# Expert weights split by pairs in three equal blocks beside the attention, with a third query buffer and unrolled heads

## The chip, the core and the metric

The kernel runs on one core of a Trainium2 chip (trn2). The metric is the device time of one launch in microseconds (us), lower is better. TensorE is PE in the profile, VectorE is DVE, ScalarE is ACT, GpSimd is POOL, and SyncE is SP. SP only issues DMAs here. All outputs are float32.

## What is computed

The model has four parts in a row, each behind a layernorm and with a residual sum: attention, a mixture of 32 experts, a state space layer and a feed forward layer with weights from a table. The change lies in the first part, which also prepares the weights of the second:

```python
# attention, x is (2, 1024, 512), 16 heads of 32
q = jnp.einsum('btc,hcd->bhtd', x, Wq) + bq[None, :, None, :]
k = jnp.einsum('btc,hcd->bhtd', x, Wk) + bk[None, :, None, :]
v = jnp.einsum('btc,hcd->bhtd', x, Wv) + bv[None, :, None, :]
scores = jnp.einsum('bhtd,bhsd->bhts', q, k) * scale
probs = jax.nn.softmax(scores + causal, axis=-1)
y = jnp.einsum('bhts,bhsd->bhtd', probs, v)
return y.transpose(0, 2, 1, 3).reshape(Bn, Tn, H * D) @ Wo + bo
# experts, 32 of them, 8 per token, inner size 192
g = jnp.einsum('th,eih->tei', x, w_gate_proj)
u = jnp.einsum('th,eih->tei', x, w_up_proj)
h = jax.nn.silu(g) * u * masked_w[:, :, None]
out = jnp.einsum('tei,ehi->th', h, w_down_proj)
```

To keep float32 accuracy on TensorE, a matrix is split into a high part (rounded to the fp32r type) and a low part (what is left). The expert weights need this once each, and that is the work that GpSimd does during the attention.

## The kernel before

The launch is a row of stages, and each is a block in which every engine has its own program. A stage ends when all its engines have ended. `attention` (L226) has three: `norm_and_project` (layernorm, then q, k and v; the parts of q and k go to DRAM), `attend` (L491, all 16 heads) and `output_projection` (L893). Only `attend` changes, apart from the order in which the host lays out the expert weights.

**TensorE, VectorE and ScalarE in `attend`.** A unit is a head, with both batches. A body is two heads, and the engines loop over six of the eight bodies; the first and the last are written out. For a head TensorE computes the scores twice. In `rows` (L709) a token's scores lie along the free dimension of the PSUM tile `ps_r`, and VectorE takes their maximum (L838). In `columns` (L739) the scores lie turned, in `ps_c`, and ScalarE takes the exponential of them (L808). Between the two, the maxima are joined and split by VectorE (L846, L850, L852), turned by TensorE (L720, L728) and put into spare rows of the query tile `q_st` by ScalarE (L797), so that the second product comes with the maximum subtracted. `output` (L752) multiplies by V into `ps_y`, and VectorE copies that to `y_st` in two halves of 512 tokens (`evacuate`, L860). The rows of head u+1 run between the columns of head u, so TensorE is a head ahead with them. There are 24 pieces of each kind in a head.

**SyncE.** It loads q and k of head u+2 into the same two buffers while head u runs, in four steps: low half of q after four of the twelve column steps, low half of k after eight (`after_column`), upper halves of both after the last. Each step is two DMAs, one of 64 partitions and one of 32. Then it waits until both halves of y are in `y_st` and stores them (`store`, L667 and L668, four DMAs). VectorE waits for all four before it writes the first half of the next head (`y_stored`). SyncE also loads the output weights `wo` ahead of the last body (L690).

**GpSimd.** It goes through the 32 experts, two for each head. For one expert it

- splits gate and up: a cast of 128x1536 to the high part (L588), a subtraction for the low part (L591), a store of both to DRAM (L594, 1536 KB), a load of the same part of the expert after next (L567, 768 KB),
- splits down: two casts of 128x512 (L607, L608), a subtraction (L611), a subtraction on the lower 64 partitions, whose rows hold the 64 rest rows of the expert a second time (L614), a store (L617, 768 KB), a load (L570, 512 KB).

Ahead of the two experts of a head it copies V of this head into `v_pair` (`take_v`, L577), once TensorE has ended the head before the last. After the last expert it splits `wo` (L637, L640) and waits for its stores. All these DMAs are issued by GpSimd itself, in order with its arithmetic.

The order on each engine is that of the code. DMAs of GpSimd run in queue q0, those of SyncE in q1.

Of the kernel before, what the change touches and what calls it, by code (L numbers as in the profile page):

```python
# [6 lines left out]
F32 = mybir.dt.float32  # L7
I32 = mybir.dt.int32
ALU = mybir.AluOpType
# [3 lines left out]
P = 128  # L13
N_TOK = 2048
D = 512
# [475 lines left out]
def attend(nc, qk, v_rows, yT, all_sums, w_raw, w_split, wo, wo_hi, wo_lo):  # L491
# [13 lines left out]
    RING = 4  # L505
    BUFS = 3
# [3 lines left out]
    GU, DN = W_GU, W_RAW - W_GU  # L510
# [3 lines left out]
    with ExitStack() as ctx:  # L514
        sb = lambda n, s, dt=F32: ctx.enter_context(nc.sbuf_tensor(n, s, dt))
        q_st, k_st = [sb(f"q_st{b}", [P, BATCH, T], F32R) for b in range(E)], [sb(f"k_st{b}", [P, BATCH, T], F32R) for b in range(E)]
        v_pair = [sb(f"v_pair{b}", [P, TILES, VW]) for b in range(E)]
        probs = [[sb(f"probs{a}{b}", [P, HALF]) for b in range(RING)] for a in range(BATCH)]
        y_st, raw_wo = sb("y_st", [P, T]), sb("raw_wo", [P, KD, D])
# [5 lines left out]
        raw_gu, raw_dn = [sb(f"e_raw_gu{x}", [P, GU]) for x in range(2)], [sb(f"e_raw_dn{x}", [P, DN]) for x in range(2)]  # L525
        gu_parts, dn_parts = [sb(f"e_gu_parts{x}", [P, 2 * GU], F32R) for x in range(2)], sb("e_dn_parts", [P, 3 * D], F32R)
# [4 lines left out]
        low_loaded, q_up_loaded, k_up_loaded = [[sem(f"{n}_loaded{b}") for b in range(E)] for n in ("qk_low", "q_up", "k_up")]  # L531
        consts, rows_done, max_done, joined, parts_done, turned, shift_ready, cols_done, exp_done, v_ready, pv_done, y_done, y_stored, turns_begun, loads_begun, warmed = [
            sem(n) for n in ("att_consts", "rows_done", "max_done", "max_joined", "max_parts_done", "max_turned", "shift_ready", "cols_done", "exp_done", "v_ready",
                             "pv_done", "y_done", "y_stored", "v_turns_begun", "q_loads_begun", "exp_warmed")]
        gu_loaded, dn_loaded = [sem(f"e_gu_loaded{x}") for x in range(2)], [sem(f"e_dn_loaded{x}") for x in range(2)]
        gu_stored, dn_stored = [sem(f"e_gu_stored{x}") for x in range(2)], sem("e_dn_stored")
        gu_split, dn_split = sem("e_gu_split"), sem("e_dn_split")
# [7 lines left out]
        def _(pool):  # L545
# [4 lines left out]
            pool.memset(raw_gu[0][:, :T], 0.0).then_inc(consts, 1)  # L550
            pool.memset(raw_gu[1][:, :T], 1.0).then_inc(consts, 1)
# [3 lines left out]
            pool.affine_select(out=raw_gu[1][:, :T], in_=raw_gu[1][:, :T], compare_op=ALU.is_ge, fill=0.0,  # L555
# [8 lines left out]
            start = lambda it, e: isinstance(it, int) and it == 0 and e == 0  # L564

            def load_gu(p, x):
                pool.dma_start(raw_gu[x][:, :], w_raw[bass.ds(p, 1), :, :GU].rearrange("e p c -> p (e c)")).then_inc(gu_loaded[x], 16)  # L567

            def load_dn(p, x):
                pool.dma_start(raw_dn[x][:, :], w_raw[bass.ds(p, 1), :, GU:].rearrange("e p c -> p (e c)")).then_inc(dn_loaded[x], 16)  # L570

            def take_v(it, e):
                u = unit(it, e)
                if not (isinstance(it, int) and it == 0):
                    pool.wait_ge(pv_done, (u - 1) * PER_UNIT + BATCH * RING)
                    pool.sem_inc(turns_begun, 1)
                nc.gpsimd.tensor_copy(v_pair[e][:, :, :DH], v_rows[:, :, bass.ds(u * DH, DH)]).then_inc(v_ready, 1)  # L577

            def split_gate_up(it, e, x, final):
                u = unit(it, e)  # L580
                p = u * 2 + x
                hi = gu_parts[x][:, :GU]
                pool.wait_ge(gu_loaded[x], u * 16 + 16)
                pool.sem_inc(turns_begun, 1)
                if not start(it, e):
                    pool.wait_ge(gu_stored[x], u * 16)
                    pool.sem_inc(turns_begun, 1)
                nc.gpsimd.tensor_copy(hi, raw_gu[x][:, :]).then_inc(gu_split, 1)  # L588
                pool.wait_ge(gu_split, p * 2 + 1)
                pool.sem_inc(turns_begun, 1)  # L590
                nc.gpsimd.tensor_tensor(gu_parts[x][:, GU:], raw_gu[x][:, :], hi.bitcast(F32), ALU.subtract).then_inc(gu_split, 1)  # L591
                pool.wait_ge(gu_split, p * 2 + 2)
                pool.sem_inc(turns_begun, 1)
                pool.dma_start(w_split[bass.ds(p, 1), :, :2 * GU].rearrange("e p c -> p (e c)"), gu_parts[x][:, :].bitcast(F32)).then_inc(gu_stored[x], 16)  # L594
                if not final:
                    load_gu(p + 2, x)

            def split_down(it, e, x, final):
                u = unit(it, e)
                p = u * 2 + x  # L600
                hi, lo, rest = dn_parts[:, :D], dn_parts[:, D:2 * D], dn_parts[:, 2 * D:]
                pool.wait_ge(dn_loaded[x], u * 16 + 16)
                pool.sem_inc(turns_begun, 1)
                if not (start(it, e) and x == 0):
                    pool.wait_ge(dn_stored, p * 16)
                    pool.sem_inc(turns_begun, 1)
                nc.gpsimd.tensor_copy(rest, raw_dn[x][:, D:]).then_inc(dn_split, 1)  # L607
                nc.gpsimd.tensor_copy(hi, raw_dn[x][:, :D]).then_inc(dn_split, 1)  # L608
                pool.wait_ge(dn_split, p * 4 + 2)
                pool.sem_inc(turns_begun, 1)  # L610
                nc.gpsimd.tensor_tensor(lo, raw_dn[x][:, :D], hi.bitcast(F32), ALU.subtract).then_inc(dn_split, 1)  # L611
                pool.wait_ge(dn_split, p * 4 + 3)
                pool.sem_inc(turns_begun, 1)
                nc.gpsimd.tensor_tensor(rest[REST_E:, :], raw_dn[x][REST_E:, D:], rest[REST_E:, :].bitcast(F32), ALU.subtract).then_inc(dn_split, 1)  # L614
                pool.wait_ge(dn_split, p * 4 + 4)
                pool.sem_inc(turns_begun, 1)
                pool.dma_start(w_split[bass.ds(p, 1), :, 2 * GU:].rearrange("e p c -> p (e c)"), dn_parts[:, :].bitcast(F32)).then_inc(dn_stored, 16)  # L617
                if not final:
                    load_dn(p + 2, x)

            def body(it, final):
                for e in range(E):
                    take_v(it, e)
                    for x in range(2):
                        split_gate_up(it, e, x, final and e == E - 1)
                        split_down(it, e, x, final and e == E - 1)

            for x in range(2):
                load_gu(x, x)
                load_dn(x, x)  # L630
            body(0, False)
            with pool.Fori(1, BODIES - 1) as it:
                body(it, False)
            body(BODIES - 1, True)
            pool.wait_ge(wo_loaded, 16)
            pool.sem_inc(turns_begun, 1)
            nc.gpsimd.tensor_copy(wo_hi[:, :, :], raw_wo[:, :, :]).then_inc(wo_split, 1)  # L637
            pool.wait_ge(wo_split, 1)
            pool.sem_inc(turns_begun, 1)
            nc.gpsimd.tensor_tensor(wo_lo[:, :, :], raw_wo[:, :, :], wo_hi[:, :, :].bitcast(F32), ALU.subtract).then_inc(wo_split, 1)  # L640
            for x in range(2):
                pool.wait_ge(gu_stored[x], 16 * HEADS)
# [2151 lines left out]
```

## Times and profile before

| | us |
|---|---|
| median of three runs | 2579.88 (2578.06 to 2584.63) |
| the profiled execution | 2575.64 |
| its span in the profile | 2574.1 |
| `attend`, first instruction of GpSimd to the end of its last | 172.2 to 628.5 |
| first instruction of `output_projection` on SyncE | 631.3 |
| granted TensorE clock over the whole span | 0.945 |

The profile shows one execution. A row of the timeline gives start, length, engine, line, operation, output and input, how many instructions are merged in it, and in brackets how long the engine sat idle before it and who ended that. A row of the waits gives who waited for whom, the sum, the count and the longest. A row of the stretches gives its length and the busy time of each engine in it with the count of instructions, then the granted clock (1.00 is 2.4 GHz, 0.50 is 1.2 GHz), the mean busy share of the 16 DMA engines and the bytes that they moved per second.

### The profile page before, as it was taken

To read this page: it belongs to the slowest core of one execution; us is meant where nothing else is said; L and a number is where in the kernel's file an instruction comes from. 1 tells how busy PE (TensorE), PEld (TensorE's weight loads), DVE (VectorE), ACT (ScalarE), POOL (GpSimd) and SP (SyncE) were. 2 spreads that over 40 slices of the span, in tenths; PEclk is the share of its full clock that TensorE was granted. 3 is DMA by queue.
4 is the path that set the end of the run, shared out by engine and by line. 5 is a ranking of instruction groups with operands and counts; after the bars stand their busy time and mean duration, and the time that the engine had idled before them with its cause. 6 is when DMAs were issued, how large, how long until landed. Compare 5 with 4: busy or idle time off the path is not lost. (4 is left out here: it accounts for less than half of the span.)

```text
span 2574.1 us, 47582 instructions
## 1 busy us (share of the span) xinstructions
PE 2334.5 (91%) x12710; PEld 1773.7 (69%) x12712; DVE 1497.5 (58%) x3155; ACT 977.3 (38%) x2202; POOL 1094.5 (43%) x993
## 2 busy tenths in 40 slices
PE   7969998996756999999999779999989998999998
PEld 5855455443535989989989648888855664788886
DVE  6336556663566555555555457999256665655554
ACT  3114555453254444444444342222255553312221
POOL 3128888776002666666667501111166663000000
PEclk9978999998866999999999879999999999999999
DMA  5458999996355999999999834447499761000001
GB/s 178 122 175 311 346 338 329 341 326 252 116 204 145 245 283 281 258 265 273 271 263 221 149 129 148 168 163 232 141 217 225 166 151 38 13 25 25 25 9 66
DMA packets 263307, 491.18 MB, mean 191 GB/s; under 512 B 31889, under 2 KB 149137, under 8 KB 253458
## 3 DMA queue, kind: packets, MB, share of 16 engines
q1 hardware_dynamic: 197202, 272.17, 34.9%
q0 software_dynamic: 62976, 212.42, 29.4%
q10 hardware_dynamic: 3024, 5.29, 0.6%
q8 instruction: 54, 0.88, 0.1%
q14 instruction: 51, 0.42, 0.1%
HBM read 592.96 MB, written 198.79 MB: 308 GB/s over the span
## 5 line engine op out<-in xcount | busy, mean ns | idle before, releaser
L1431 PE MATMUL m_ps_u<-m_ring,m_xT_hi 128*128 x1280 | 370.4, 350 | 0.2 <-issue 0.2
L1399 POOL DMA_INDIRECT expert_sum<-x_res,token_of x160 | 257.1, 1607 | 182.9 <-DMA expert_sum<-x_res,token_of 66.3
L808 ACT ACTIVATE probs<-ps_c 128x512 f32<-128x512 f32 (+3 forms) x384 | 179.1, 491 | 208.7 <-PE ps_c L741 102.7
L1431 PEld LDWEIGHTS m_ps_u<-m_ring,m_xT_hi 128*128 128x128 f32 x1280 | 236.7, 190 | 1.2 <-issue 0.6
L1431 PE MATMUL m_ps_u<-m_ring,m_xT_lo 128*128 x640 | 216.9, 339 | 0.0
L1392 POOL DMA_INDIRECT m_xg<-x_rows,token_of x160 | 172.5, 1078 | 100.6 <-issue 92.3
L709 PE MATMUL ps_r<-k_st,q_st 96*128 96x512 f32 (+3 forms) x384 | 163.8, 433 | 53.4 <-DVE neg_max L838 22.4
L1878 PE MATMUL s_ps<-s_x_hi,s_w_hi 128*128 128x512 f32 x512 | 199.7, 390 | 1.6 <-POOL s_w_lo L1848 1.6
L1878 PE MATMUL s_ps<-s_x_lo,s_w_hi 128*128 128x512 f32 x512 | 199.3, 389 | 0.0
L1878 PE MATMUL s_ps<-s_x_hi,s_w_lo 128*128 128x512 f32 x512 | 199.2, 389 | 0.0
L2647 DVE TENSOR_TENSOR x_res<-f_ps_o,x_res 128x512 f32<-128x512 f32 x176 | 109.3, 684 | 143.4 <-PE f_ps_o L2540 143.4
L1557 DVE SCALAR_TENSOR_TENSOR m_h<-m_silu,m_xg,m_ps_u 128x128 f32<-128x128 f32 x160 | 55.7, 348 | 234.1 <-ACT m_silu L1496 194.4
L1450 PE MATMUL m_ps_y<-m_ring,m_hT_hi 128*128 x480 | 176.9, 423 | 6.6 <-issue 6.6
L838 DVE TENSOR_REDUCE neg_max<-ps_r 128x1 f32<-128x512 f32 (+3 forms) x256 | 138.1, 584 | 70.7 <-PE ps_r L709 37.2
L1926 ACT ACTIVATE s_out<-s_ps 128x512 f32<-128x512 f32 x128 | 76.4, 598 | 254.1 <-PE s_ps L1878 254.1
L739 PE MATMUL ps_c<-q_st,k_st 128*128 128x512 f32 (+3 forms) x384 | 159.0, 418 | 0.6 <-ACT probs L808 0.5
L752 PE MATMUL ps_y<-probs,v_pair 128*33 128x512 f32 (+3 forms) x768 | 159.2, 539 | 0.0
L1846 POOL CAST s_w_hi<-s_raw 128x512 fp32r<-128x512 f32 x32 | 21.7, 677 | 308.0 <-PE s_ps L1878 215.6
L1496 ACT ACTIVATE m_silu<-m_ps_u 128x192 f32<-128x192 f32 x160 | 52.9, 330 | 239.2 <-PE m_ps_u L1431 194.0
L2260 PE MATMUL s_ps_o<-s_w_out_sb,gated 128*128 128x512 f32 x256 | 126.8, 623 | 5.1 <-DVE gated L2387 4.0
L709 PEld LDWEIGHTS ps_r<-k_st,q_st 96*128 96x128 f32 x384 | 81.3, 212 | 71.2 <-DVE neg_max L838 35.1
L1502 ACT COPY x_res<-m_ps_y 128x512 f32<-128x512 f32 x160 | 94.0, 588 | 95.6 <-PE m_ps_y L1450 84.3
(357 smaller groups left out, 5782.0 us busy)
## 6 DMA issues: line engine op xcount, KB each, us to landing
m_ring<-w_split SPq DMA_DIRECT2D x160, 1536.0 KB
m_ring<-w_split SPq DMA_DIRECT2D x160, 768.0 KB
w_split<-e_gu_parts POOLq DMA_DIRECT2D x32, 1536.0 KB
proj<-s_out SPq DMA_DIRECT2D x32, 1024.0 KB, 4.0
e_raw_gu<-w_experts POOLq DMA_DIRECT2D x32, 768.0 KB
w_split<-e_dn_parts POOLq DMA_DIRECT2D x32, 768.0 KB
e_raw_dn<-w_experts POOLq DMA_DIRECT2D x32, 512.0 KB
q_st<-q_parts SPq DMA_DIRECT2D x32, 256.0 KB
```

The source lines that it names most:

```text
L709: last = nc.tensor.matmul(ps[:, :w], q_st[e][:K_QK, a, tb * P:(tb + 1) * P], k_st[e][:K_QK, a, c:c + w], start=True, stop=not diagonal)
L739: last = nc.tensor.matmul(ps[:, :width], k_st[e][:, a, s * P:(s + 1) * P], q_st[e][:, a, t0:t0 + width], start=True, stop=not diagonal)
L752: nc.tensor.matmul(ps_y[a * COL:a * COL + VW, t0 % HALF:t0 % HALF + width], v_pair[e][:, a * TB + s, :], probs[a][j % RING][:, :width], st ...
L808: nc.scalar.activation(probs[a][j % RING][:, :width], ps_c[(j * BATCH + a) % BUFS][:, :width], ACT.Exp, scale=SCALE).then_inc(exp_done, 1)
L838: nc.vector.tensor_reduce(dst, ps_r[n % BUFS][:, :w], AX.X, ALU.max, negate=True).then_inc(max_done, 1)
L1392: pool.indirect_dma_start(xg[j % X_TURNS][:, :], None, x_rows, rows_at(j), bounds_check=PADDED - 1, oob_is_err=True).then_inc(x_loaded[j % ...
L1399: pool.indirect_dma_start(acc[j % 2], rows_at(j), y[j % TURNS], None, bounds_check=PADDED - 1, oob_is_err=True, compute_op=ALU.add).then_i ...
L1431: last = nc.tensor.matmul(ps_u[b % 2][:, :W_UP], x[b % 2][:, k, :], ring[:, first + k * GU_ROW:][:, bass.ds(place, W_UP)], start=(n == 0), ...
L1450: last = nc.tensor.matmul(ps_y[b % 2][:, :], a[b % 2][:, c, :], ring[:, first:][:, bass.ds(place, D)], start=(n == 0), stop=(n == len(term ...
L1878: last = nc.tensor.matmul(ps[g][:, :], w[:, k, :], x[:, k, of_group(g)], start=(n == 0), stop=(n == 3 * KD - 1))
L2260: last = nc.tensor.matmul(ps_o[tt][:, :], gated[b][:, k, tt * P:(tt + 1) * P], w_o[:, k, :], start=(k == 0), stop=(k == KO - 1))
L2647: nc.vector.tensor_tensor(x_res[:, i, :], ps_o[s][:, :], x_res[:, i, :], ALU.add).then_inc(added, 1)
```

## The change

1. The host lays out the expert weights by pairs: `w_experts[u]` has three blocks of 128x1536 float32, gate and up of expert 2u, gate and up of expert 2u+1, and the down weights of both. In the third the 64 rest rows of the one expert lie over the 64 of the other, so nothing is held twice.
2. GpSimd works by these blocks, once per head: casts of blocks 0 and 1, subtractions of 0 and 1, store and reload of 0, store and reload of 1; then cast, subtraction, store and reload of block 2. The store of block 2 is four DMAs: the main rows of each expert, 512 KB each, from two places of the tile, and the rest rows, high parts in one and low parts in the other, 256 KB each, to two experts at once. Each block has one raw buffer, one buffer of parts, and its own semaphores.
3. `raw_wo` now lies over the raw blocks. GpSimd loads `wo` itself after the last store and splits it after waiting for all stores and for this load.
4. There are three query buffers (`Q_BUFS`). Both halves of q of head u+3 are loaded after head u. k keeps its two buffers and its two moments.
5. y is stored in two halves, each as soon as it is in `y_st`, with a semaphore for each half, and VectorE waits for that half of the head before.
6. SyncE, TensorE, ScalarE and VectorE have no loop over the bodies any more. GpSimd still loops.

The core of the diff:

```diff
-            def split_gate_up(it, e, x, final):
...
-            def split_down(it, e, x, final):
...
+            def split_high(u, x, first):
+                pool.wait_ge(w_loaded[x], u * 16 + 16)
+                pool.sem_inc(turns_begun, 1)
+                if not first:
+                    pool.wait_ge(w_stored[x], u * STORES[x] * 16)
...
+                nc.gpsimd.tensor_copy(high[x], raw[x]).then_inc(high_done, 1)
...
+            def store_down(u):
+                pool.wait_ge(low_done, u * UNITS_OF_PAIR + 3)
...
+                for x in range(2):
+                    dst = w_split[bass.ds(2 * u + x, 1), :, 2 * W_GU:2 * W_GU + 2 * D].rearrange("e p (n c) -> p (e n) c", n=2)
+                    pool.dma_start(dst, parts_all[:, 2, :, x * D:(x + 1) * D].bitcast(F32)).then_inc(w_stored[2], 16)
+                for n in range(2):
+                    dst = w_split[bass.ds(2 * u, 2), n * REST_E:(n + 1) * REST_E, 2 * W_GU + 2 * D:]
+                    pool.dma_start(dst, parts_all[:, 2, n, 2 * D:].bitcast(F32)).then_inc(w_stored[2], 16)
+
+            def split_pair(u, first, more):
+                split_high(u, 0, first)
+                split_high(u, 1, first)
+                split_low(u, 0)
+                split_low(u, 1)
+                for x in range(2):
+                    store_gate_up(u, x)
+                    if more:
+                        load_raw(u + 1, x)
+                split_high(u, 2, first)
+                split_low(u, 2)
+                store_down(u)
+                if more:
+                    load_raw(u + 1, 2)
...
+            pool.dma_start(raw_wo, wo.rearrange("(k p) d -> p k d", p=P)).then_inc(wo_loaded, 16)
+            for x in range(UNITS_OF_PAIR):
+                pool.wait_ge(w_stored[x], HEADS * STORES[x] * 16)
             pool.wait_ge(wo_loaded, 16)
...
+            for u in range(HEADS):
+                if u + E < HEADS:
+                    sp.wait_ge(cols_done, u * PER_UNIT + 8 * BATCH)
+                    load_k(u + E, 0)
+                store_y(u, 0)
+                if u + E < HEADS:
+                    sp.wait_ge(cols_done, (u + 1) * PER_UNIT)
+                    load_k(u + E, 1)
+                store_y(u, 1)
+                if u + Q_BUFS < HEADS:
+                    for half in range(2):
+                        load_q(u + Q_BUFS, half)
...
-                if half == 0:
-                    dve.wait_ge(y_stored, (u + 1) * 64)
+                dve.wait_ge(y_stored[half], (u + 1) * 64)
```

What GpSimd runs, as the compiled program has it (the operation, output and input by name, the shape, and how many alike in a row). Before, from the copy of V for a head to the first cast of its second expert:

```order
L577 COPY v_pair<-v_rows 128x16x32
L588 CAST e_gu_parts<-e_raw_gu 128x1536
L591 TENSOR_TENSOR e_gu_parts<-e_raw_gu,e_gu_parts 128x1536
L594 DMA w_split<-e_gu_parts 128x3072
L567 DMA e_raw_gu<-w_experts 128x1536
L607 CAST e_dn_parts<-e_raw_dn 128x512
L608 CAST e_dn_parts<-e_raw_dn 128x512
L611 TENSOR_TENSOR e_dn_parts<-e_raw_dn,e_dn_parts 128x512
L614 TENSOR_TENSOR e_dn_parts<-e_raw_dn,e_dn_parts 64x512
L617 DMA w_split<-e_dn_parts 128x1536
L570 DMA e_raw_dn<-w_experts 128x1024
```

And now, a whole pair, from the copy of V on:

```order
L571 COPY v_pair<-v_rows 128x16x32
L579 CAST e_parts<-e_raw 128x1536 x2
L584 TENSOR_TENSOR e_parts<-e_raw,e_parts 128x1536 x2
L592 DMA w_split<-e_parts 128x3072
L587 DMA e_raw<-w_experts 128x1536
L592 DMA w_split<-e_parts 128x3072
L587 DMA e_raw<-w_experts 128x1536
L579 CAST e_parts<-e_raw 128x1536
L584 TENSOR_TENSOR e_parts<-e_raw,e_parts 128x1536
L600 DMA w_split<-e_parts 128x2x512 x2
L603 DMA w_split<-e_parts 2x64x512 x2
L587 DMA e_raw<-w_experts 128x1536
```

The first store of a pair now stands behind two casts and two subtractions, and two stores have a first dimension of 2.

What SyncE issues for one head in the steady state. Before, in the loop, from the low half of q to the first store of y:

```order
L651 DMA q_st<-q_parts 64x2x512
L651 DMA q_st<-q_parts 32x2x512
L658 REGISTER_ALU
L655 DMA k_st<-k_parts 32x2x512
L655 DMA k_st<-k_parts 64x2x512
L658 REGISTER_ALU
L651 ISA
L651 DMA q_st<-q_parts 64x2x512
L651 DMA q_st<-q_parts 32x2x512
L655 DMA k_st<-k_parts 32x2x512
L655 DMA k_st<-k_parts 64x2x512
L663 ISA
```

And now, from the low half of k to the upper half of k:

```order
L654 DMA k_st<-k_parts 32x2x512
L654 DMA k_st<-k_parts 64x2x512
L661 DMA yT<-y_st 32x512
L662 DMA prob_sums<-y_st 1x512
L661 DMA yT<-y_st 32x512
L662 DMA prob_sums<-y_st 1x512
L654 DMA k_st<-k_parts 32x2x512
L654 DMA k_st<-k_parts 64x2x512
```

The first half of y is stored ahead of the upper half of k; the second half of y and then all of q, for the head after next but one, follow behind it.

## Rows read from the trace of the kernel before

**Rows 1.** Timeline of GpSimd at the end of the stage.

```profile
598.25 0.61 POOL L577 COPY v_pair<-v_rows 128x512 f32<-128x512 f32 x1
...
621.37 0.57 POOL L617 DMA_DIRECT2D w_split<-e_dn_parts  x1 [0.60 <-POOL e_dn_parts L614]
621.99 1.89 POOL L637 CAST wo_hi<-raw_wo 128x2048 fp32r<-128x2048 f32 x1
624.06 4.49 POOL L640 TENSOR_TENSOR wo_lo<-raw_wo,wo_hi 128x2048 fp32r<-128x2048 f32 x1 [0.18 <-POOL wo_hi L637]
```

**Rows 2.** Timeline of SyncE at the end of the stage.

```profile
626.13 0.28 SPq L668 DMA_DIRECT2D prob_sums<-y_st  x1
631.31 0.36 SPq L925 DMA_DIRECT2D o_sums<-prob_sums  x1
```

**Rows 3.** Timeline of GpSimd, start and one expert in full.

```profile
182.47 0.62 POOL L567 DMA_DIRECT2D e_raw_gu<-w_experts  x1 [4.17 <-DVE k_st L829]
...
189.97 1.47 POOL L588 CAST e_gu_parts<-e_raw_gu 128x1536 fp32r<-128x1536 f32 x1 [4.68 <-DMA e_raw_gu<-w_experts]
...
215.29 0.61 POOL L577 COPY v_pair<-v_rows 128x512 f32<-128x512 f32 x1
...
256.20 1.47 POOL L588 CAST e_gu_parts<-e_raw_gu 128x1536 fp32r<-128x1536 f32 x1
257.85 3.44 POOL L591 TENSOR_TENSOR e_gu_parts<-e_raw_gu,e_gu_parts 128x1536 fp32r<-128x1536 f32 x1 [0.18 <-POOL e_gu_parts L588]
262.06 0.56 POOL L594 DMA_DIRECT2D w_split<-e_gu_parts  x1 [0.76 <-POOL e_gu_parts L591]
262.67 0.55 POOL L567 DMA_DIRECT2D e_raw_gu<-w_experts  x1
```

**Rows 4.** Waits between 180 and 625 us: who, for whom, sum, times, longest.

```profile
DVE y_st L860 <- DMA prob_sums<-y_st: 19.9, 13, 3.8
...
POOL e_dn_parts L607 <- DMA w_split<-e_dn_parts: 7.8, 10, 1.3
```

**Rows 5.** Waits of TensorE between 197 and 625 us.

```profile
PE ps_r L709 <- DVE neg_max L838: 22.4, 17, 2.9
PE ps_r L709 <- DMA q_st<-q_parts: 9.6, 7, 2.3
```

**Rows 6.** Stretches: one fast head, the steady part, the end of the stage.

```profile
282.00:306.00 24.00, 23.17 (x139) 12.89 (x137) 14.73 (x31) 13.62 (x29) 20.41 (x20) 1.00 0.97 350
...
230.00:600.00 370.00, 337.64 (x1824) 178.18 (x1825) 229.50 (x418) 189.26 (x391) 300.18 (x284) 0.94 0.96 338
600.00:629.00 29.00, 23.66 (x136) 11.14 (x132) 6.07 (x12) 13.89 (x34) 24.74 (x18) 0.95 0.60 233
```

**Rows 7.** DMA queues between 230 and 600 us: packets, MB, share of 16 engines.

```profile
q0 software_dynamic: 15513, 98.93, 70.4%
q1 hardware_dynamic: 13924, 25.88, 25.3%
```

**Rows 8.** Timeline of VectorE, then of GpSimd, in one head.

```profile
412.38 1.28 DVE L850 CAST max_cols<-neg_max 128x8 fp32r<-128x8 f32 x1
...
420.24 3.38 DVE L852 TENSOR_TENSOR max_cols<-neg_max,max_cols 128x8 fp32r<-128x8 f32 x1
...
413.00 0.62 POOL L608 CAST e_dn_parts<-e_raw_dn 128x512 fp32r<-128x512 f32 x1
...
420.16 3.43 POOL L591 TENSOR_TENSOR e_gu_parts<-e_raw_gu,e_gu_parts 128x1536 fp32r<-128x1536 f32 x1 [0.18 <-POOL e_gu_parts L588]
```

**Rows 9.** Timeline of TensorE around a wait for a query load.

```profile
422.15 0.79 PE L709 MATMUL ps_r<-k_st,q_st 96*128 96x512 f32 x1 [2.29 <-DMA q_st<-q_parts]
...
431.24 0.40 PE L709 MATMUL ps_r<-k_st,q_st 96*128 96x512 f32 x1
```

**Rows 10.** A short stretch in the first stage, with stores of 4x32x512 by SyncE.

```profile
102.20:102.60 0.40, 0.40 (x4) 0.32 (x3) 0.40 (x1) 0.00 (x0) 0.00 (x0) 1.00 0.24 87
```

**Rows 11.** The page's DMA issues: a store with its time to landing.

```profile
proj<-s_out SPq DMA_DIRECT2D x32, 1024.0 KB, 4.0
```

More of the change, by code:

```diff
@@ L563, in _, with take_v @@
             pool.wait_ge(consts, CONSTS)
[L564 to L574, printed above, removed]
+            def take_v(u, h, first):
+                if not first:
@@ L621, in body @@
[L621 to L631, printed above, removed]
-            with pool.Fori(1, BODIES - 1) as it:
-                body(it, False)
-            body(BODIES - 1, True)
+                nc.gpsimd.tensor_tensor(low[x], raw[x], high[x].bitcast(F32), ALU.subtract).then_inc(low_done, 1)
@@ L653, in load_k @@
[L653 removed]
+                    sp.dma_start(q_st[u % Q_BUFS][row * DH:(row + j - i) * DH, :, half * HALF:(half + 1) * HALF].bitcast(F32), part("q", u, i, j, half)).then_inc(loaded, 16)
+            def load_k(u, half):
+                loaded = (k_low_loaded, k_up_loaded)[half][u % E]
                 for row, i, j in ((0, 0, 1), (1, 0, 2)):
[L655 removed]
@@ L682, in _ @@
[L682 to L692 removed]
+                    sp.dma_start(k_st[u % E][row * DH:(row + j - i) * DH, :, half * HALF:(half + 1) * HALF].bitcast(F32), part("k", u, i, j, half)).then_inc(loaded, 16)
@@ L694, in _ @@
+            for half in range(2):
+                sp.wait_ge(y_stored[half], 64 * (HEADS + 1))
         @block.tensor
@@ L781, in _ @@
                     turn_lower(0, 0)
-            body(0, True, False)
-            with pe.Fori(1, BODIES - 1) as it:
-                body(it, False, False)
-            body(BODIES - 1, False, True)
+            for it in range(BODIES):
+                body(it, it == 0, it == BODIES - 1)
             outputs(BODIES - 1, E - 1, NCH - 2)
@@ L815, in _ @@
             shift(0, 0, 0)
-            with act.Fori(0, BODIES - 1) as it:
-                body(it, False)
-            body(BODIES - 1, True)
+            for it in range(BODIES):
+                body(it, it == BODIES - 1)
         @block.vector
@@ L885, in _ @@
             parts(0, 0, 1)
-            body(0, True, False)
-            with dve.Fori(1, BODIES - 1) as it:
-                body(it, False, False)
-            body(BODIES - 1, False, True)
+            for it in range(BODIES):
+                body(it, it == 0, it == BODIES - 1)
             evacuate(BODIES - 1, E - 1, 1)
```

174 lines of the change are left out of this document (75 added, 99 removed).

## The prediction

> **What bounds the kernel now.** The launch is a row of stages and the change touches one, `attend`. So I ask only when this stage ends; what comes behind it moves with it. The first view is the timeline at its end. GpSimd's last instruction there starts at 624.06 and takes 4.49 us, so it ends at 628.55 [rows 1]. SyncE issues the last store of y at 626.13, and the next stage's first load goes out at 631.31 [rows 2]. Both strands end within a few us, GpSimd's last.
>
> The second view is GpSimd's timeline. The copies of V stand at 215.29 and 598.25, which is 14 heads, so a head takes it (598.25 - 215.29) / 14 = 27.35 us [rows 1, 3]. Its waits for DMAs are 7.8 us in the whole stage [rows 4]: it runs at the pace of its own instructions.
>
> The third view is the waits of the attention itself. TensorE waits 22.4 us for maxima and 9.6 us for query loads [rows 5], VectorE 19.9 us for the store of y [rows 4]. A wait costs more than its length: after the one of 2.29 us a product of 512 columns takes 0.79 us and nine us later 0.40 [rows 9], the two levels of TensorE's clock (1.2 and 2.4 GHz). A head with none of it took 24.0 us at a clock of 1.00 [rows 6].
>
> The fourth view is the DMA engines: busy 96% of the time between 230 and 600 us, at 338 GB/s, and 97% in the fast head [rows 6]. The page gives no one this bound, since nobody waits long for it; but it says how much room is left.
>
> **The queries, y and the unrolling.** Loading q a head earlier and storing y by halves takes away up to 9.6 + 19.9 us of waits and the slow clock behind them. The best that TensorE can come to is 24.0 us a head. This counts only if GpSimd gets below 27.35 too, because the stage ends with both. So these edits cost and give nothing by themselves; they decide that GpSimd is the one to look at. The loads of k keep their moments. The unrolling takes away a branch per body; no wait on one is among the rows, so 0, and at most a few us of instruction loading either way, off the path in any case.
>
> **GpSimd's own work.** A pair is now a copy of V (0.61), three casts (1.47 each), three subtractions (3.44 each), nine DMAs (0.56 each), and the waits of 0.18 and 0.76 between cast, subtraction and store once, for block 2; in blocks 0 and 1 other instructions lie between [rows 1, 3]. That is 0.61 + 4.41 + 10.32 + 5.04 + 0.94 = 21.3 us instead of 27.35. Over 15 heads this would be 90 us. It can't be had, for the next reason.
>
> **The DMA engines.** One MB of q0 takes 370 x 0.704 / 98.93 = 2.63 us of all 16 engines, one of q1 370 x 0.253 / 25.88 = 3.62 [rows 7]. A head had 2 x (1536 + 768 + 768 + 512) KB = 7.34 MB of weights and 1.84 MB of q, k and y: 19.3 + 6.7 = 26.0 us, 95% of 27.35, as the row says. Now it has 2 x 1536 + 1536 of stores and 3 x 768 of loads, 6912 KB = 7.08 MB: 18.6 + 6.7 = 25.3 us. So no head can take less than about 25.3.
>
> Can it come to that? Before, the next part was loaded some 20 us ahead of its use. Now there is a loop. Block 1 must have landed; then come its cast and the two subtractions, 1.47 + 2 x 3.44 = 8.35 us; then store 0, load 0, store 1, load 1 are issued within 2 us and run one behind the other in one queue: 4608 KB = 4.72 MB, 12.4 us; and the last of them is block 1 for the next head. To this comes a delay from issue to landing. A store of 1.05 MB landed after 4.0 us [rows 11], 1.2 over its bytes; the first load here after 7.5 us [rows 3], 5.4 over its 2.1, beside other loads. The steady case is nearer to the first: I take 2. And q1 takes its share of the engines in these 14 us: between 0 and 6.7, I take 2.8, a little under its mean share. Loop: 8.35 + 2 + 12.4 + 2.8 = 25.55 us.
>
> **The stores of the rest rows.** They go to two experts, first dimension 2 [the order of the change]. With stores of 4x32x512 in flight from SyncE alone, 0.24 of the 16 engines were busy, four, at 87 GB/s, so 22.7 GB/s each [rows 10]. I read this as: a first dimension of 4 spreads a store over four engines. Then one of 2 puts 262 KB on two engines, 131 KB / 22.7 = 5.8 us on each, where the mean over 16 would be 0.7. By the Trainium skill (DMA: Bandwidth & Descriptors, "Why a DMA increments its semaphore by 16 and not by 1") the number of engines is the largest up to 16 that divides both slowest dimensions, and for GpSimd's DMAs the group moves on from one DMA to the next; the row agrees with the first half of this, no row here shows the second. Without the spread rule the loop above would stand at 25.55.
>
> On a loaded engine the cycle is 25.3 - 1.4 + 5.8 = 29.7 us against 25.55 for the loop, so the next head's last load lands up to 4.1 us late; if the pair moves on, the engine is clear again one head later, and every second head pays: 0 to 2.1 us a head. Part is worked off while q1 sends nothing, so I take 1.45. **A head of GpSimd: 27.0 us**, between 25.3 and 29.7.
>
> **The start and the end.** The first load lands at 189.97 as before [rows 3], the second with 2.1 us of bytes and its share by 193. So the first store goes out at 193 + 8.35 = 201.4. From the 16th such store to the end of the stage there are no reloads: block 2 follows (1.47 + 0.18 + 3.44 + 0.76 and issues, 7 us), its four stores 2.4, then the load of `wo` at +9.4. It queues behind the two stores of 3.15 MB (8.3 and 2 of delay), block 2 (1.57 MB, 4.1, on the loaded engines 4.8 more), then itself 2.8: +22. Then 1.89 + 0.18 + 4.49 = 6.6 us of splitting [rows 1]: +28.5. Before, `wo` was long there. And the last three heads have no loads of q and k, 2 us less each.
>
> Sum: 201.4 + 15 x 27.0 + 28.5 - 6 = 628.9, against 628.55. The saved 0.35 us a head (15 times, 5 us) is given back by the later load of `wo`. The profiled execution would come to 2575.64 + 0.4 = 2576; it lay 4.2 us under the median, so the median would be 2579.88 + 0.4 = **2580 us**.
>
> **Rival A, the head comes down to the DMA bound.** The two-engine stores cost nothing, because other engines' idle time covers them, and q1 gets out of the way. Then a head takes 25.3 to 26.3 us, with 25.8 a stage end of 201.4 + 387 + 22.5 = 610.9, which is 18 us less: 2562. For it: 96% busy shows that the engines can be kept that full, and TensorE at 24.0 leaves room [rows 6]. Against it: they were kept full by requests 20 us ahead, which are gone.
>
> **Rival B, the two-engine stores cost in every head.** If the two engines are the same each time, or both stores of a pair fall on them, a head can't take less than 29.7 us: 15 x 2.7 = 40 us more, 2620; if only part of it comes through, 28.2 a head, 2598. It decides as soon as the backlog of an engine is still there when the next store 0 is issued, that is, from 25.55 - (25.3 - 1.4) = 1.7 us of surplus on.
>
> **Rival C, VectorE is locked out and TensorE becomes the bound.** A cast of 8 columns took 1.28 us while GpSimd's two casts ran, the latter from 413.00 to 413.62, and a subtraction of 8 columns 3.38 us beside GpSimd's of 3.43 from 420.16 [rows 8]. It ended when GpSimd's instruction ended, and in the first case not between two without a gap. The Trainium skill (SBUF — State Buffer, "Who interferes with whom") says that the two engines share a pair of ports, which the first holds for its whole instruction; the rows agree. Now two casts and two subtractions stand without a gap, 2 x 1.47 + 2 x 3.44 = 9.8 us. TensorE needs these small operations twice a head. With a chance of 9.8 / 27 each and 4.9 us on the mean: 3.5 us a head, and about 1 more for the slow clock: 24.0 + 4.5 = 28.5. That passes 27.0 and gives 15 x 1.5 = 22 us more: 2603. Against it: TensorE falls into a place where the long stretch misses these operations, or loses only what it would wait for GpSimd anyway. It decides where the delay is over 3 us a head.
>
> That the change doesn't do what it says: GpSimd issued its DMAs itself before too [rows 3], so nothing comes from that part.
>
> **How the numbers follow.** A measurement of this kernel can tell about 0.3%, 8 us, from no change, which is half a us per head here. The forecast, 26.5 to 27.5 a head, has 0.38. Rival A has 0.33, since 1.2 us of my head are a guess about how shares fall. Rival B has 0.17, Rival C 0.12. Faster is A: 0.33; within 0.3%: 0.38; slower is B and C: 0.29. The range takes in the better part of A and the partial forms of B and C: 2557 to 2602. It leaves out a head at the bare DMA bound with a short end, and B in full.
>
> **What would show it.** GpSimd should wait some 5 us a head for the load of block 1 or for stores of block 2, where it waited 0.5. Its copies of V should stand 27.0 us apart, the first store at about 201, and between the last store and the cast of `wo` a gap of some 11 us that was none. TensorE's waits for q and VectorE's for the store of y should be gone, and TensorE should wait for V or sit idle ahead of the end. The prediction is wrong if the copies of V stand 25.5 apart (A), if the waits for block 2's stores are longest (B), or if TensorE waits for maxima over 3 us a head while GpSimd waits for TensorE (C).

## The result and the profile after

| | before | after | ratio, 95% |
|---|---|---|---|
| median, us | 2580.2 | 2601.1 | 1.0075 (1.005 to 1.010) |
| again, beside the experiments | 2576.1 | 2596.8 | 1.0075 (1.0049 to 1.0101) |
| span of the profiled execution | 2574.1 | 2592.3 | |
| last instruction of GpSimd in `attend` ends | 628.55 | 636.52 | |
| SyncE's first load of the next stage | 631.31 | 640.74 | |
| expert stage, first to last instruction of GpSimd | 661.9 | 674.0 | |

The kernel is slower by 21 us in the median and by 18.2 in the profiled executions: 9.4 up to the next stage's first load, 12.1 in the expert stage, and about 3 come back in the stages behind.

GpSimd's timeline after, as [rows 1, 3]:

```profile
203.08 0.57 POOL L592 DMA_DIRECT2D w_split<-e_parts  x1
...
214.72 0.62 POOL L571 COPY v_pair<-v_rows 128x512 f32<-128x512 f32 x1
...
273.60 1.47 POOL L579 CAST e_parts<-e_raw 128x1536 fp32r<-128x1536 f32 x1 [4.58 <-DMA e_raw<-w_experts]
...
286.33 1.46 POOL L579 CAST e_parts<-e_raw 128x1536 fp32r<-128x1536 f32 x1 [2.31 <-DMA e_raw<-w_experts]
...
591.60 0.62 POOL L571 COPY v_pair<-v_rows 128x512 f32<-128x512 f32 x1
...
604.88 1.18 POOL L592 DMA_DIRECT2D w_split<-e_parts  x2
...
614.91 0.81 POOL L632 DMA_DIRECT2D e_raw<-wo  x1
629.96 1.89 POOL L637 CAST wo_hi<-e_raw 128x2048 fp32r<-128x2048 f32 x1 [14.23 <-DMA e_raw<-wo]
632.03 4.49 POOL L640 TENSOR_TENSOR wo_lo<-e_raw,wo_hi 128x2048 fp32r<-128x2048 f32 x1 [0.18 <-POOL wo_hi L637]
```

The copies of V stand (591.60 - 214.72) / 14 = 26.92 us apart, the first stores of a pair (604.88 - 203.08) / 15 = 26.79. Two waits are new. One of 2.8 to 4.7 us stands ahead of block 1's cast in every head from 240 us on (273.60). The other, ahead of block 2's (286.33), comes in some heads: of the 14 such casts between 231 and 582 us, nine waited 0.5 to 3.6 us. The sum of both, and the waits of TensorE (between 180 and 625, and 197 and 625 us, as [rows 4, 5]):

```profile
POOL e_parts L579 <- DMA e_raw<-w_experts: 79.4, 26, 7.4
...
PE ps_r L706 <- DVE neg_max L832: 17.5, 16, 3.9
PE ps_r L706 <- issue: 10.4, 8, 2.9
```

The waits for q and for the store of y are gone. TensorE still loses 10.4 us at the starts of heads, which the page names "issue" because it finds no releaser; another such wait is in the fence on VectorE below. The steady part, as [rows 6], then DMA packets and queues of the same stretch, as [rows 7]:

```profile
230.00:600.00 370.00, 347.31 (x1884) 188.77 (x1882) 245.10 (x428) 185.87 (x395) 287.91 (x219) 0.93 0.93 333
```

```profile
DMA packets 43227, 123.06 MB, mean 333 GB/s; under 512 B 17040, under 2 KB 17040, under 8 KB 39658
...
q0 software_dynamic: 28615, 98.23, 73.0%
q1 hardware_dynamic: 14585, 24.49, 19.7%
```

The engines are busy 93% where it was 96. The last y is stored from 623.63, and GpSimd is 13 us behind it. Then the next stage's load (timeline of SyncE, as [rows 2]):

```profile
623.63 0.27 SPq L662 DMA_DIRECT2D prob_sums<-y_st  x1
640.74 0.36 SPq L916 DMA_DIRECT2D o_sums<-prob_sums  x1
```

The expert stage, which the change does not touch: its stretch before and after (columns as in [rows 6]), and the instruction queue on the two pages, before first.

```profile
804.30:1461.20 656.90, 640.22 (x3675) 582.55 (x3675) 356.45 (x831) 285.35 (x640) 426.46 (x318) 0.99 0.96 247
```

```profile
813.70:1482.70 669.00, 644.30 (x3675) 586.93 (x3675) 356.54 (x831) 285.54 (x640) 428.41 (x318) 0.98 0.94 243
```

```profile
q14 instruction: 51, 0.42, 0.1%
```

```profile
q14 instruction: 97, 0.79, 0.1%
```

The same 3675 products take 12 us longer, and nearly twice as many packets bring instructions: 97 for 51, and 39 of the 46 new ones lie between 900 and 1500 us.

### The profile page after: what moved, and what is told of

Same layout as the page of the kernel before. It is cut to its first block and busy times, and to the rows that moved or that the text cites. A ratio compares the mean times of both kernels' runs of the same rounds, so it can differ in the third digit from the quotient of the medians.

```text
span 2592.3 us, 45753 instructions
## 1 busy us (share of the span) xinstructions
PE 2335.3 (90%) x12710; PEld 1782.3 (69%) x12712; DVE 1514.9 (58%) x3155; ACT 969.8 (37%) x2196; POOL 1078.5 (42%) x914
## 5 line engine op out<-in xcount | busy, mean ns | idle before, releaser
L584 POOL TENSOR_TENSOR e_parts<-e_raw,e_parts 128x1536 fp32r<-128x1536 f32 x48 | 164.8, 3446 | 3.0 <-POOL e_parts L579 3.0
L1838 POOL CAST s_w_hi<-s_raw 128x512 fp32r<-128x512 f32 x32 | 21.7, 677 | 306.2 <-PE s_ps L1870 209.4
```

Of the source, the lines that this page charges most:

```text
L584: nc.gpsimd.tensor_tensor(low[x], raw[x], high[x].bitcast(F32), ALU.subtract).then_inc(low_done, 1)
```

## The experiments

Each ratio is against the kernel before on the same chip. "Loop at" is the instruction of SyncE's program at which its loop of the expert stage begins, 290 instructions long; "q14" the packets of the instruction queue; "experts" the time from the first down product of the ninth to that of the 153rd of the 160 blocks of tokens, which leaves out a start that takes 42 to 43 us in e1 to e4 and 46 to 49 in all others, whatever the kernel. e1 to e4 ran on one chip, e5 to e8 on another, e9 to e12 on a third; of before and after in the first two rows the chip isn't on record. The expectations below count the instruction packets of the whole trace, 12 to 14 more than the page.

| kernel | ratio (95%) | head, V to V | `attend`, GpSimd | next stage begins | loop at | q14 | experts |
|---|---|---|---|---|---|---|---|
| before | 1 | 27.35 | 628.6 | 631.3 | 473 | 51 | 577.9 |
| after | 1.0075 (1.005, 1.010) | 26.92 | 636.5 | 640.7 | 648 | 97 | 590.0 |
| e5, after again | 1.0075 (1.0049, 1.0101) | 26.89 | 633.6 | 637.8 | 648 | 97 | 596.1 |
| e1, SyncE unrolled | 0.9993 (0.9972, 1.0015) | 27.31 | 632.9 | 635.7 | 641 | 92 | 586.8 |
| e2, attention part alone | 0.9997 (0.9974, 1.002) | 26.86 | 621.5 | 624.2 | 649 | 98 | 588.4 |
| e3, pairs alone | 1.0183 (1.0144, 1.0222) | 29.74 | 665.9 | 675.9 | 472 | 50 | 582.9 |
| e4, after, rest by expert | 1.0001 (0.9979, 1.0023) | 26.16 | 620.5 | 627.5 | 648 | 98 | 584.8 |
| e6, e3 with rest by expert | 1.0173 (1.013, 1.0215) | 29.76 | 664.2 | 676.1 | 472 | 51 | 577.9 |
| e7, after, block by block | 1.0024 (0.9994, 1.0054) | 27.81 | 644.3 | 651.9 | 648 | 97 | 589.7 |
| e8, three repairs | 0.9938 (0.9912, 0.9964) | 24.83 | 590.5 | 597.5 | 648 | 98 | 585.8 |
| e9, after, code moved | 1.0019 (0.9995, 1.0042) | 26.96 | 636.0 | 640.2 | 729 | 57 | 582.3 |
| e10, e8, code moved by 81 | 0.9889 (0.9851, 0.9926) | 24.83 | 597.5 | 604.5 | 729 | 58 | 580.2 |
| e11, e8, code moved by 256 | 0.9933 (0.9911, 0.9956) | 24.84 | 591.9 | 598.9 | 904 | 100 | 589.3 |
| e12, e6, block by block | 0.9974 (0.9948, 0.9999) | 25.94 | 612.6 | 622.2 | 472 | 51 | 579.1 |

### One part of the change at a time

e1 is the kernel before with SyncE's loop written out:

```diff
-            with sp.Fori(0, BODIES - 1) as it:
+            for it in range(BODIES - 1):
                 body(it, False)
```

> The kernel before, with SyncE's loop over the bodies of attend written out and nothing else changed. Theory: about half of the loss (12.7 us of it) lies in the expert stage, where SyncE's own loop now stands at another place of its program and its code is loaded anew in every pass (instruction queue q14: 97 packets in the changed kernel, 51 before). Then this kernel shows over 80 packets there, the expert stage some 10 us longer, and 2588 to 2592 us in all, with attend unchanged at 628.5. Rival: the expert stage is longer because the weights lie otherwise in memory or arrive otherwise; then this kernel is equal to the one before within 3 us.

The reloads are there, 92 packets, and its 587 us in the expert stage are 9 more than in the trace of before (and 4 more than in e3, on its own chip). But its time is that of the kernel before, and its profiled execution was the slowest of its ten runs. As an account of all 12 us the theory looked weak, and I put it aside until e9.

e2 takes the third query buffer, y by halves and the unrolling, and keeps GpSimd's old program. e3 takes the pairs and keeps the old attention.

> The changed kernel with GpSimd's work of before: experts one by one, the old layout, wo loaded ahead by SyncE; kept are the three query buffers, y by halves and the written out heads. Theory: TensorE and VectorE lose their 9.6 and 19.9 us of waits, but GpSimd's 27.35 us a head stay, so attend ends at 628 within 3 us; the expert stage is 10 us longer by the code loading, so 2590 in all. Rival: TensorE was the strand that set the end, then attend ends 5 to 15 us earlier. Second rival: the written out programs do no harm to the expert stage, then 2578 to 2582.

> The kernel before with GpSimd's part of the change alone: pairs in three blocks, their layout, wo over the raw blocks; two query buffers, y in one piece and all loops stay. Theory: GpSimd's copies of V stand 26.9 us apart and wo comes late, so attend ends near 636 or some us later with the waits of TensorE that are back; the expert stage is as before (no reloading of SyncE's code, under 60 packets in q14), so 2587 to 2592. Rival (memory layout): the expert stage is 10 us longer here, so 2597 to 2602.

The attention part alone ends `attend` 7 us earlier, and the expert stage, 5 us longer than in e3, eats most of that up. GpSimd's own program is that of before, but its waits for the stores of down fell from 7.8 us [rows 4] to 0.7, so the 7 us came through the DMA engines; it waits for V neither before nor here. The pairs alone end `attend` 37 us later: the attention part of the change is what makes the pairs bearable.

### The stores of the rest rows

e4 cuts each 2x64x512 store into two of 64x512:

```diff
-                    dst = w_split[bass.ds(2 * u, 2), n * REST_E:(n + 1) * REST_E, 2 * W_GU + 2 * D:]
-                    pool.dma_start(dst, parts_all[:, 2, n, 2 * D:].bitcast(F32)).then_inc(w_stored[2], 16)
+                    for x in range(2):
+                        dst = w_split[bass.ds(2 * u + x, 1), n * REST_E:(n + 1) * REST_E, 2 * W_GU + 2 * D:].rearrange("e p c -> p (e c)")
+                        pool.dma_start(dst, parts_all[x * REST_E:(x + 1) * REST_E, 2, n, 2 * D:].bitcast(F32)).then_inc(w_stored[2], 16)
```

> The changed kernel, with the two stores of rest rows that go to two experts (2x64x512) cut into four that go to one each (64x512), same bytes. Theory: a store with a first dimension of 2 keeps two DMA engines busy for 6 us; by expert it is spread over all, the last store of block 2 lands 4 to 6 us sooner, and a head of GpSimd falls from 26.9 to 25.5 to 26.3 us, less 1.2 us for two more issues of 0.6, so 10 us less in attend or, where TensorE holds it, 3. In all 2590 to 2599 against 2601. Rival: the skew is hidden, then the head is 26.9 to 27.3 and the time the same within 3 us.

The waits between 180 and 625 us, GpSimd's end, and the packets from 230 to 600:

```profile
POOL e_parts L579 <- DMA e_raw<-w_experts: 61.1, 17, 7.3
```

```profile
593.83 1.18 POOL L592 DMA_DIRECT2D w_split<-e_parts  x2
...
613.95 1.89 POOL L638 CAST wo_hi<-e_raw 128x2048 fp32r<-128x2048 f32 x1 [8.82 <-DMA e_raw<-wo]
```

```profile
DMA packets 31609, 125.83 MB, mean 340 GB/s; under 512 B 5112, under 2 KB 5112, under 8 KB 27849
```

The wait ahead of block 2 is gone from every head (17 waits instead of 26), the step from store to store is (593.83 - 204.01) / 15 = 25.99 us instead of 26.79, and the wait for `wo` is 8.8 us instead of 14.2. That makes 12 us in the heads and 5 in the tail: 16 us of `attend` hang on the form of these two stores, with two issues more on GpSimd. In the kernel after, the DMA engines between 281 and 283.5 us, while block 2's load, issued at 266.40, is still out (its cast begins at 286.33), were in tenths of 16 engines:

```profile
DMA  5343142411441131411227012240033399913209
```

A few engines work on, most have nothing to do, and the load isn't complete. The view doesn't say which engines these are.

### Block by block, and the load of `wo` ahead

e7 casts, subtracts, stores and reloads block 0, then block 1:

```diff
-                split_high(u, 0, first)
-                split_high(u, 1, first)
-                split_low(u, 0)
-                split_low(u, 1)
                 for x in range(2):
+                    split_high(u, x, first)
+                    split_low(u, x)
                     store_gate_up(u, x)
```

> The changed kernel, but each block is cast, subtracted, stored and reloaded before the next: the request for block 1 has only 2.4 MB queued ahead of it instead of 4.7, and GpSimd never has two casts and two subtractions in a row. If the loop cast, subtraction, four transfers, next cast sets the head (25.99 us without the two-engine stores, 26.79 with them): the wait for block 1 all but goes, a head takes 25.3 to 26.3 us, attend ends 8 to 20 us earlier (617 to 629). If the DMA engines' bytes with the two-engine stores set it: 26.5 to 27.0 a head, no gain. If VectorE's lock was what held TensorE, its two operations of 3.4 us in a row at the start of heads go, and TensorE's waits for maxima fall from 17.5 to under 10 us.

GpSimd's waits for loads all but went (7.6 us in 3), and yet a head took 27.8 us: now it waits for TensorE to end a head, before it may copy the next V. First this wait, between 180 and 640 us, then TensorE's waits between 197 and 660 us, and the longest of them:

```profile
POOL v_pair L571 <- PE ps_y L747: 48.0, 10, 11.1
```

```profile
PE ps_r L704 <- issue: 35.3, 9, 10.2
PE ps_r L704 <- DVE neg_max L830: 10.5, 15, 1.9
```

```profile
598.41 0.77 PE L704 MATMUL ps_r<-k_st,q_st 96*128 96x512 f32 x1 [10.15 <-issue]
```

These are the starts of heads, where by its program TensorE waits for nothing but maxima and the loads of q and k. So I read the waits called "issue" as late loads; the page doesn't name them. GpSimd now issues faster, and the backlog falls on q and k. The runs spread from 2566 to 2620 us.

e8 has the same order, the rest by expert as in e4, and the load of `wo` right behind the second store of the last pair (the wait for all stores now stands behind the splitting of `wo`):

```diff
+                if not more:
+                    pool.dma_start(raw_wo, wo.rearrange("(k p) d -> p k d", p=P)).then_inc(wo_loaded, 16)
                 split_high(u, 2, first)
```

> The changed kernel with the rest rows stored by expert, block by block, and the output weights loaded after the last pair's second store instead of after its sixth. Stores by expert gave 16 us in attend. Added: a head of 25.3 to 25.8 us instead of 25.99 (bound by the bytes: 3 to 10 us) and a tail without the wait of 8.8 us for the output weights (5 to 8 us). Attend should end at 603 to 613, the time should be 2557 to 2567 (ratio 0.992 to 0.996). If TensorE or GpSimd's own 21 us and waits for V take over, the head stays at 26 and only the tail comes: 614, 2568.

```profile
230.00:570.00 340.00, 323.42 (x1859) 177.61 (x1859) 233.21 (x423) 182.34 (x390) 296.87 (x248) 0.98 1.01 357
```

```profile
583.91 1.89 POOL L635 CAST wo_hi<-e_raw 128x2048 fp32r<-128x2048 f32 x1 [0.35 <-DMA e_raw<-wo]
```

A head of 24.83 us, DMA engines without a gap at 357 GB/s, no wait for `wo`; `attend` ends 46 us earlier than after and better than expected. GpSimd in one head:

```profile
437.14 3.45 POOL L584 TENSOR_TENSOR e_parts<-e_raw,e_parts 128x1536 fp32r<-128x1536 f32 x1 [0.19 <-POOL e_parts L579]
...
462.69 1.47 POOL L579 CAST e_parts<-e_raw 128x1536 fp32r<-128x1536 f32 x1
464.35 3.48 POOL L584 TENSOR_TENSOR e_parts<-e_raw,e_parts 128x1536 fp32r<-128x1536 f32 x1 [0.19 <-POOL e_parts L579]
468.58 0.58 POOL L592 DMA_DIRECT2D w_split<-e_parts  x1 [0.76 <-POOL e_parts L584]
```

Between 230 and 570 us it waits for no load, no store and no V. Most heads take 24.7 us, and that is its own instructions: the 21.3 us of the prediction, two issues more (1.1) and the waits of 0.18 and 0.76 in blocks 0 and 1 too (1.9) make 24.3. So GpSimd is at its own pace again, with the DMA engines full beside it. Between e7 and e8 the head differs by 3 us, the load of `wo` has no part in a head, and GpSimd's waits for V, 48.0 us or 3.2 a head in e7, are none in e8: where the engines have no slack, the two-engine stores cost 3 us a head instead of 0.8.

### The old attention with the pairs

> The old attention loop (two query buffers, loops) with the weights by pairs, and each rest store cut into two stores of one expert, 64 rows each, as in the experiment that did this to the changed kernel. Pairs on the old attention cost 37 us in attend, with 16 us of waits for q and 16 for k. If the two-engine stores hold the loads of q and k back: waits for q and k together fall under 15 us, attend ends at 628 to 640 and the time is 2572 to 2590. If it is the burst of requests and the blocked VectorE, whatever the store's form: waits for maxima stay at 30 us, attend ends at 655 or later, and the time stays over 2605.

> The old attention loop with the weights by pairs and the rest rows by expert, now block by block. The same without the new order took 2618 us, with 31 us of waits for maxima and 22 us for k. If the burst of two stores and two loads in one queue makes k late: the waits for k fall under 8 us and attend ends at 628 to 645. If the blocked VectorE is the cause: the waits for maxima fall under 20 us and those for k stay over 15; attend ends at 640 to 655. If neither, since the old attention waits for its own two query buffers: it stays at 660 or more.

TensorE's waits between 197 and 660 us in e6, then in e12:

```profile
PE ps_r L703 <- DVE neg_max L832: 30.8, 14, 7.4
PE ps_r L703 <- DMA k_st<-k_parts: 21.7, 12, 4.4
```

```profile
PE ps_r L701 <- DVE neg_max L830: 24.3, 11, 5.1
PE ps_r L701 <- DMA q_st<-q_parts: 6.0, 5, 1.8
PE ps_r L701 <- DMA k_st<-k_parts: 3.1, 4, 1.4
```

That the two-engine stores were behind the 37 us fell with e6: the time stayed, and the waits for q and k together went from 32.3 us in e3 only to 26.1. With the transfers spread out (e12), `attend` ended 52 us earlier, the waits for k fell from 21.7 to 3.1 us, and GpSimd's waits for V from 86.8 us (12 times) to 15.4 (7 times): in e6 TensorE set the head. The order of the blocks did that. It changes two things at once: two stores and two loads, 4.7 MB, are no longer issued in one piece ahead of the load of k, and GpSimd's two subtractions no longer stand in a row. The waits for maxima fell by 6.5 us alone, so I take the burst for the larger part; no run parts the two.

### The expert stage

> The changed kernel itself once more, beside the experiments. Two accounts of where its 21 us come from. The first: 8 us in the stage attend, whose mechanism is the store of the rest rows on two engines, and 12 us in the expert stage, which always come with it: then the expert stage takes 673 to 675 us again and the time is 1.006 to 1.010 of the kernel before. The second: the 8 us in attend are its own, the expert stage's are an accident of the execution, since two kernels with the same code loading (104 to 112 instruction packets) took 664 and 666 there: then the expert stage takes 662 to 667, and the time is 1.002 to 1.005.

It is no accident: 596 us, long again. e9, e10 and e11 add instructions that do nothing to SyncE's program in `attend`, where it would wait:

```diff
+            for _ in range(81):
+                sp.sem_inc(padded, 1)
             for u in range(HEADS):
```

> The changed kernel with 81 instructions more on SyncE (increments of a semaphore that nobody reads, in a place where SyncE would wait for TensorE). In every kernel with unrolled SyncE code the instruction queue fetched some 8 packets per 100 us in the expert stage, where it had been one; SyncE's loop there has 290 instructions and began at its instruction 473 before, at 641 to 649 in the unrolled kernels. With 81 more it begins at 729, which is 473 + 256. If the place of the loop against blocks of code decides: the instruction queue falls from 109 packets to about 65, and the expert stage takes 8 to 12 us less (662 to 670 instead of 674 to 680), the time is 1.002 to 1.005 of the kernel before. If it is the length of the code, or the packets cost nothing: 105 packets or more, or the expert stage stays at 672 to 680, the time at 1.0075.

> The kernel with the three repairs, and the same 81 instructions. If the place of SyncE's loop decides: about 65 packets, expert stage 658 to 664 instead of 669.5, time 8 to 10 us under that of the three repairs alone, so 2547 to 2550 beside 2576 (ratio 0.988 to 0.991). If not: ratio 0.994 as before.

> The control: 256 instructions instead of 81, so that the loop begins at 904, which has the same place against blocks of 128 or 256 instructions as in the kernel with the three repairs. If the place decides: 105 packets or more again, and a time like the three repairs alone (ratio 0.994). If any added instructions help, or the length decides: as with 81, or more packets still.

The instruction queue between 1000 and 1400 us in after, e9, e10 and e11:

```profile
q14 instruction: 33, 0.27, 0.2%
```

```profile
q14 instruction: 3, 0.02, 0.0%
```

```profile
q14 instruction: 5, 0.04, 0.0%
```

```profile
q14 instruction: 35, 0.29, 0.2%
```

81 instructions more, and the reloads are gone; 256 more, and they are there as with none. So neither the length of the program nor the added instructions decide, but the place of the loop, and a shift by 256 leaves it as it was. In after a pass of this loop takes some 66 us and brings 5 to 9 packets of 8192 B, which begin right behind the branch: it lies at 1008.3 and 1071.9 us, the packets at 1009.0 and 1073.1. In the kernel before a pass has none or one, once two. In e9 the expert stage's 3675 products take:

```profile
812.90:1472.90 660.00, 639.51 (x3675) 583.24 (x3675) 355.46 (x831) 284.59 (x640) 426.00 (x318) 0.99 0.96 245
```

That is 9 us less than after, and the waits of TensorE for the ring of weights (7.9 us, 3 times, in after) are gone. The new layout of the weights is not the cause: e3, e6 and e12 have it, and no reloads. Over all kernels the stage's part in the table is 578 to 583 us without reloads and 585 to 596 with them; by chip the difference is 2 to 6 us (e1, e2, e4 against e3), 8 to 18 (e5, e7, e8 against e6) and 7 to 10 (e11 against e9, e10, e12). e5 and e9 differ by 0.56% (1.0075 and 1.0019, on two chips), e10 and e11 by 0.44% on one chip, though there the intervals overlap.

## Why the prediction was right and where it was wrong

The time lay inside the range by 0.9 us, but the likeliest case, no change that can be told, was wrong: 0.75% slower. That it lay inside is in part luck. The range reached to 2602 for partial forms of Rivals B and C in `attend`; 12 us of the measured 21 came from a stage that the prediction left out. Step by step:

- **The head**: 27.0 predicted, 26.92 measured. Of its terms the loop was 25.55 and is 25.99 (e4); the two-engine stores were 1.45 and are 0.8 (e4 against after). That they are paid in some heads and not in others is what the waits ahead of block 2 show. One error covered the other.
- **The first store**: 201.4 predicted, 203.08 measured, 1.7 us.
- **The tail**: 28.5 predicted, 636.52 - 604.88 = 31.6 measured. The two-engine part was right (4.8 against 5.0); `wo` landed 3 us later than sized even without it (20.1 us behind the last pair's first store in e4, against 17.2), and the wait ahead of its cast was 14.2 us, not 11.
- **Three heads without loads, -6 us**: this step failed. The last step between stores is 604.88 - 578.23 = 26.65. The loads that fall away are those of q1; the loop of q0 sets the head and keeps its length.
- **The sum for `attend`**: 1.7 - 15 x 0.21 + 3.1 + 6 = 7.7 us over 628.9; measured 636.5.
- **TensorE can come to 24.0 a head**: not here. Its joins of maxima stand 27.07 us apart (25.1 in e8); I read that as late halves of k at head starts. But GpSimd never waits for V in after, and the last y lies 13 us ahead of GpSimd's end, so TensorE didn't set the stage.
- **The DMA bound, 25.3 a head, "no head can take less"**: wrong as a bound, by 0.5 us. e8 ran at 24.83 with the same bytes. Its own packets give 7.08 x 2.60 + 1.84 x 3.72 = 25.2 us by the same working, at a share of 1.01: the times of packets can add up to more than the engines' time, so their sum is no floor. What the floor is stays open.
- **Rival B** (two-engine stores in every head) is not this kernel. e7 comes near it, with 27.8 us, but by another path: through TensorE and the wait for V. **Rival A** is the way to e8: engines kept full, but only with requests spread out and the stores by expert.
- **Rival C**: the lock is there (below), but waits for maxima fell from 22.4 [rows 5] to 17.5 us.
- **"What comes behind moves with it", and "the unrolling: 0, off the path in any case"**: this was the costliest step, 12 of the 18 us. I looked for the price of unrolled code where it runs. It is paid 200 us later, in a loop that the unrolling moved. Without it (e9) the change stands at 1.0019 (0.9995 to 1.0042), which is the likeliest case of the prediction.

VectorE and GpSimd in one head (timelines), and TensorE's product behind them:

```profile
384.57 3.37 DVE L844 CAST max_cols<-neg_max 128x8 fp32r<-128x8 f32 x1
387.98 3.37 DVE L846 TENSOR_TENSOR max_cols<-neg_max,max_cols 128x8 fp32r<-128x8 f32 x1
...
384.49 6.83 POOL L584 TENSOR_TENSOR e_parts<-e_raw,e_parts 128x1536 fp32r<-128x1536 f32 x2
...
387.15 0.76 PE L706 MATMUL ps_r<-k_st,q_st 96*128 96x512 f32 x1 [2.94 <-issue]
```

Two operations on 8 columns last 3.37 us each, one beside each of GpSimd's two subtractions: the first ends, GpSimd's next has begun, and the second waits again. Such a pair comes once in the stage. Of the 64 small operations 11 last over 2 us, where it was 5 of 64 before: the loss is more frequent, and still small.

Open: why the same reloads cost 2 to 6 us on one chip and up to 18 on another, and 586 to 596 us on one chip with the same place of the loop. The small price on their chip is in line with e1 and e2, which are no slower as a whole. The fastest kernel is e10: 2550.8 us, 1.1% faster than before.

## What to carry to other kernels

A transfer's first dimension is part of its price: two stores with 2 there cost 0.8 us a head where the engines had slack and 3 us where they had none. Requests in one burst can also delay the small loads of another queue, so split, store and reload block by block; but with the two-engine stores left in, the same order made a head longer (26.9 to 27.8 us), so mend those first. And when code is unrolled, look at the instruction queue of the later stages, before and after: if a loop elsewhere begins to be fetched in each pass, move it.

## What the runs showed of the hardware

**Reloads.** A loop of 290 instructions ran from what was loaded when it began at 472, 473 or 729, and was fetched again in every pass when it began at 641 to 649 or at 904, at 2 to 18 us a stage, as the table shows. The places are those in the compiled program. The Trainium skill (Runtime: NRT & Kernel Launch, "Instruction fetch mechanics") says that an engine holds two blocks of 256 instructions, and that a taken branch to a place outside of them makes it wait for a fetch. By that rule the loop fits when it touches two blocks, and a shift by 256 changes nothing; e11 agrees with that. Whether the places themselves agree no run here shows: the trace has 322 records of SyncE in a pass, 32 moves more than the compiled program's 290, so places there need not be places in the engine's memory. The same section calls this a reason to unroll; here unrolling one stage brought it on in another.

**Stores on two engines.** After has 17040 packets under 512 B from 230 to 600 us, e4 has 5112. In the whole of `attend` the trace of after has 14336 packets of 8 bytes in q0, which is 448 for each of the 32 stores with first dimension 2; e7 has as many, and before, e4 and e8 have none. A store of 262 KB in packets of 4096 B is 32 for each of two engines, and 14 x 32 = 448: it looks as if each idle engine gets an empty packet for every full one. That, and that it is two engines, is an inference from the count; no view names a packet's engine. The small packets took 9 ns each, which spread over 16 engines is 7 us in these 370, or half a us a head. So of the 0.8 us a part may be theirs and not that of the two crowded engines; no run parts them.
